# Layer 3's self-attention in a nine-stage transformer kernel: one set of statistics for both norms, one key or query block a unit, other tasks spread out

## The reference, cut to what matters

```
def _layernorm(x, eps=1e-05):
    m = jnp.mean(x, axis=-1, keepdims=True)
    v = jnp.var(x, axis=-1, keepdims=True)
    return (x - m) / jnp.sqrt(v + eps)
# B 8 batches of N 256 tokens, D = 128, H = 16 heads of DK = 8 columns
xx = _layernorm(x)
y = ln1(xx)                                  # again mean and variance, then * ln1_w + ln1_b
q, k, v = split(y @ w_qkv)
attn = softmax(einsum('bhnd,bhmd->bhnm', q, k) * (1.0 / sqrt(DK)))
s = xx + einsum('bhnm,bhmd->bhnd', attn, v) @ w_proj
# a mixture of eight MLPs on s follows, in the next stage
```

## Time and profile before

| | us |
|---|---|
| three runs: median (lowest to highest) | 4559.78 (4558.39 to 4569.89) |
| the profiled execution, its own time | 4569.0 |
| the profiled execution, span from first to last instruction | 4567.2 |
| of it the stage L3s, from its first instruction to its last VectorE instruction | 272 |

### The profile page before, as it was taken

One profiled execution on the slowest core, in us unless ns is written; L12 is line 12 of the kernel. 1 busy time (PEld: TensorE's weight loads), 2 busy tenths in 40 slices (PEclk: granted clock), 3 DMA queues, 4 the chain that ended last, 5 costly groups with the idle time before them and its releaser, 6 DMA issues. The chain is left out here.

```text
span 4567.2 us, 74534 instructions
## 1 busy us (share of the span) xinstructions
PE 4165.2 (91%) x26475; PEld 2849.5 (62%) x26508; DVE 2802.0 (61%) x6502; ACT 2573.6 (56%) x4381; POOL 127.1 (3%) x153
## 2 busy tenths in 40 slices
PE   7797999999789999999999999779999999967889
PEld 6564454454467777777777777446666666644557
DVE  7655888786566665556565555555555555547656
ACT  6423667666256666666666667334444444436457
POOL 2100000000000000000000000000000000000000
PEclk9898999999889999999999999889999999988989
DMA  2101433230110000000000000020000000000010
GB/s 75 51 5 52 68 52 46 48 43 15 37 40 13 5 12 5 15 3 15 2 15 13 4 1 4 24 61 8 9 9 9 9 2 2 2 19 3 8 59 8
DMA packets 118722, 99.10 MB, mean 22 GB/s; under 512 B 12020, under 2 KB 111508, under 8 KB 117244
## 3 DMA queue, kind: packets, MB, share of 16 engines
q1 hardware_dynamic: 112588, 87.28, 8.6%
q10 hardware_dynamic: 5760, 6.92, 0.4%
HBM read 62.85 MB, written 12.58 MB: 17 GB/s over the span
## 5 line engine op out<-in xcount | busy, mean ns | idle before, releaser
L1240 DVE CUSTOM_DVE_ANT_0 L2a_sc<-L2a_score,L2a_mask_n 128x804 f32<-128x804 f32 x512 | 498.9, 991 | 101.1 <-issue 77.7
L1157 ACT ACTIVATE L2a_pt<-L2a_ring 128x512 f32<-128x512 f32 x768 | 431.3, 599 | 203.9 <-PE L2a_ring L1054 202.3
L621 ACT ACTIVATE L1a_work<-L1a_ring 128x1024 f32<-128x1024 f32 x416 | 413.5, 1028 | 173.5 <-PE L1a_ring L439 172.4
L741 DVE TENSOR_REDUCE L1a_mx<-L1a_ring 128x2 f32<-128x1024 f32 x384 | 456.6, 1222 | 66.1 <-PE L1a_ring L458 62.0
L2187 PE MATMUL L3a_res<-L3a_probs,L3a_n 128*128 128x512 f32 (+1 forms) x960 | 489.5, 592 | 0.0
L2280 ACT ACTIVATE L3a_probs<-L3a_ring 128x512 f32<-128x512 f32 (+1 forms) x480 | 279.7, 590 | 309.8 <-PE L3a_ring L2076 305.1
L1054 PE MATMUL L2a_ring<-L2a_ident,L2a_sc 128*128 128x128 f32 x3072 | 443.3, 283 | 5.7 <-ACT L2a_sc L1144 1.9
L1144 ACT ACTIVATE L2a_sc<-L2a_sc,L2a_nb 128x1608 f32<-128x1608 f32 x256 | 417.8, 1634 | 0.7 <-DVE L2a_nb L1245 0.7
L2397 DVE TENSOR_REDUCE L3a_mx<-L3a_ring 128x1 f32<-128x402 f32 (+2 forms) x640 | 316.4, 538 | 152.4 <-PE L3a_ring L2154 143.0
L1054 PEld LDWEIGHTS L2a_ring<-L2a_ident,L2a_sc 128*128 128x128 f32 x3072 | 350.6, 144 | 79.9 <-issue 43.7
L1069 PE MATMUL L2a_res<-L2a_pt,L2a_v 128*64 128x256 f32 (+1 forms) x3328 | 373.4, 381 | 1.7 <-ACT L2a_pt L1157 1.7
(11 more groups left out here) (749 smaller groups left out, 7994.2 us busy)
## 6 DMA issues: line engine op xcount, KB each, us to landing
L1a_keys<-L1a_k_hi SPq DMA_DIRECT2D x224, 52.0 KB
L1a_cx<-in_ctx SPq DMA_DIRECT2D x8, 768.0 KB
L2a_cx<-in_ctx SPq DMA_DIRECT2D x8, 768.0 KB
L1a_keys<-L1a_k_lo SPq DMA_DIRECT2D x112, 52.0 KB
L0a_cx<-in_ctx SPq DMA_DIRECT2D x16, 320.0 KB, 3.5
L3a_cx<-in_ctx SPq DMA_DIRECT2D x16, 320.0 KB, 3.8
L2a_mask_u<-in_mask SPq DMA_DIRECT2D x16, 200.1 KB, 4.4
L1a_scr_q<-L1a_keys SPq DMA_DIRECT2D x3, 1024.0 KB
```

The source lines that it names most:

```text
L621: act.activation(probs[:, (par * NU + u) % c.PS, :, :], ring[tile][:, :, :], ACT.Exp).then_inc(tile_free[tile], 1)
L741: dve.tensor_reduce(mx[:, g % 2, hf, one, :, ch], ring[tile][:, :, :], AX, ALU.max).then_inc(tile_free[tile], 1)
L1157: ins = act.activation(pt[:, t:t + 4, g // 3, q], bank[:, :].rearrange("p (t q) -> p t q", t=4), ACT.Copy)
L1240: dve.tensor_tensor_reduce(sc[:, two, e, w].rearrange("p (k j) -> p k j", k=2), score[e][:, :, 0:CH], mask_n[:, r % 2, w].rearrange("p (k ...
```

## The change

It has these parts:

- Statistics of `x` are taken once, block by block. From mean and variance GpSimd works out both factors: `1/sqrt(var + EPS)` for `xx`, and for `y` in one step `1/sqrt(var * (1 + EPS) + EPS * EPS)`, which is what two norms in a row come to. `norm` writes `y` directly from `x`. `xx` is written by GpSimd in a new task `resid`, a batch at a time, when `finish` will soon want it.
- Blocks 1, 2 and 3 get their statistics and `norm` at different times: block 1 in units 0 and 1, block 2 in 5 and 6, block 3 in 13 and 14.
- `key` and `query` have no part on VectorE any more; that part is a task of its own, `key_lo` or `query_lo`, which stands in the next unit, behind `rows`. From unit 8 on there is one projection a unit, in units 2 to 5 also, and two in units 6 and 7.
- Ahead of unit 0 only groups 0 to 2 of block 0 are projected; group 3 and `value` of block 0 stand in unit 0.
- The tasks of a finished batch stand ahead of `rows` instead of at the third places: `denominator`, `spread (b, 0)`, `spread (b, 1)`, `project` in one unit each, and `finish` in the next one.
- Clearing `v` moves from VectorE to GpSimd, and VectorE takes block 0's statistics ahead of its wait for the weights.

```diff
 def __init__(self):
...
-        for s in ("stats", "rsqrt", "norm", "stats_2", "rsqrt_2", "norm_2"):
+        for s in ("stats", "scale", "norm", "turn"):
             put(s, 0)
-        put("turn", 0)
-        for g in range(self.NG):
+        for g in range(3):
             put("key", (0, g))
             put("query", (0, g))
...
+        for g in range(2):
+            put("key_lo", (0, g))
+            put("query_lo", (0, g))
+        put("tops", (0, 0))
+        put("tops", (0, 1))
+        put("shift", 0)
+        put("key_lo", (0, 2))
+        put("query_lo", (0, 2))
         put("rows", 0)
...
+    def projected(self, u):
+
+        block, at = divmod(u, 8)
+        if u < 0 or block + 1 == self.NB:
+            return []
+        n = block + 1
+        if block:
+            return [(("key", "query")[at % 2], (n, at // 2))]
+        return {2: [("key", (1, 0))], 3: [("query", (1, 0))], 4: [("key", (1, 1))], 5: [("query", (1, 1))],
+                6: [("key", (1, 2)), ("query", (1, 2))], 7: [("key", (1, 3)), ("query", (1, 3))]}.get(at, [])
...
+        b, step = divmod(u - 5, 4)
+        if step == 0 and b >= 1:
+            first.append(("finish", b - 1))
         if b >= 0:
-            tasks += [[("denominator", b)], [("spread", (b, 0))], [("spread", (b, 1)), ("project", b)], [("finish", b)]][(u - 5) % 4]
-        share = lambda k: [put(*t) for t in tasks[k * len(tasks) // 3:(k + 1) * len(tasks) // 3]]
+            first += {0: [("denominator", b), ("resid", b)], 1: [("spread", (b, 0))], 2: [("spread", (b, 1))], 3: [("project", b)]}[step]
+        if n < self.NB:
+            if at == (0 if block else 2):
+                first.append(("turn", n))
+            if at == 6:
+                first.append(("value", n))
+        second += [(kind + "_lo", k) for kind, k in self.projected(u - 1)]
+        if u == 0:
+            second.append(("stats", 1))
+        elif at == 5 and n + 1 < self.NB:
+            second.append(("stats", n + 1))
+        third += self.projected(u)
+        if u == 0:
+            third += [("scale", 1), ("key", (0, 3)), ("query", (0, 3)), ("value", 0), ("key_lo", (0, 3)), ("query_lo", (0, 3))]
+        if u == 1:
+            third.append(("norm", 1))
+        if n + 1 < self.NB and at in (5, 6):
+            third.append((("scale", "norm")[at - 5], n + 1))
...
         put("scores", (u, 0))
-        share(0)
+        share(first)
         if u + 1 < self.NU:
             put("rows", u + 1)
+        share(second)
...
         put("scores", (u, 1))
-        share(1)
+        share(third)
         if ahead:
             put("shift", u + 2)
-        share(2)
...
+            def scale_of(n):
+
+                t = tokens_of(n)
+                pool.wait_ge(mv_ok, n + 1)
+                pool.tensor_scalar(var[:, 1, :], mv[:, t, 1], 1.0 + EPS, EPS * EPS, ALU.mult, ALU.add)
+                pool.tensor_scalar(var[:, 0, :], mv[:, t, 1], EPS, None, ALU.add)
+                pool.drain()
+                pool.tensor_tensor(inv[:, 1, t], var[:, 1, :], half[:, :], ALU.pow)
+                pool.drain()
+                pool.tensor_tensor(var[:, 1, :], mv[:, t, 0], inv[:, 1, t], ALU.mult)
+                pool.drain()
+                pool.tensor_scalar(off[:, t], var[:, 1, :], -1.0, None, ALU.mult).then_inc(scale_ok, 1)
+                pool.tensor_tensor(inv[:, 0, t], var[:, 0, :], half[:, :], ALU.pow)
+                pool.drain()
+                if n == 0:
+                    pool.memset(v[:, :, :], 0.0)
...
+            def resid(b):
+                for t in range(SH * b, SH * (b + 1)):
+                    ins = pool.tensor_scalar(xx[:, t, :], x[:, t, :], mv[:, t, 0:1], inv[:, 0, t:t + 1], ALU.subtract, ALU.mult)
+                ins.then_inc(xx_ok, 1)
...
             dve.memset(parts[:, :, :, :, :, :], 0.0)
-            dve.memset(v[:, :, :], 0.0)
...
```

More of the change, by code:

```diff
@@ L1333, in __init__ @@
             self.unit(u)
-        for what in (("finish", B - 2), ("values", self.NU - 1), ("result", self.NU - 1), ("denominator", B - 1), ("spread", (B - 1, 0)),
-                     ("spread", (B - 1, 1)), ("project", B - 1), ("finish", B - 1)):
+        for what in (("project", B - 2), ("values", self.NU - 1), ("result", self.NU - 1), ("denominator", B - 1), ("resid", B - 1), ("finish", B - 2),
+                     ("spread", (B - 1, 0)), ("spread", (B - 1, 1)), ("project", B - 1), ("finish", B - 1)):
             put(*what)
@@ L1342, in unit @@
         block, at = divmod(u, 8)
-        tasks = []
-        if u < 3:
-            tasks += [[("stats", 1), ("rsqrt", 1), ("norm", 1)], [("stats_2", 1), ("rsqrt_2", 1)], [("norm_2", 1), ("turn", 1)]][u]
-        if block + 1 < self.NB and (u >= 3 or block):
-            n = block + 1
-            prep = [("turn", n)] if block else []
-            for g in range(self.NG):
-                prep += [("key", (n, g)), ("query", (n, g))]
-            prep.append(("value", n))
-            first, steps = (0, 6) if block else (3, 3)
-            k = at - first
-            if k < steps:
-                tasks += prep[k * len(prep) // steps:(k + 1) * len(prep) // steps]
-        b = (u - 5) // 4
-        if b >= 0:
-            tasks += [[("denominator", b)], [("spread", (b, 0))], [("spread", (b, 1)), ("project", b)], [("finish", b)]][(u - 5) % 4]
-        share = lambda k: [put(*t) for t in tasks[k * len(tasks) // 3:(k + 1) * len(tasks) // 3]]
+        n = block + 1
+        first, second, third = [], [], []
+        b, step = divmod(u - 5, 4)
+        if step == 0 and b >= 1:
+            first.append(("finish", b - 1))
+        if b >= 0:
+            first += {0: [("denominator", b), ("resid", b)], 1: [("spread", (b, 0))], 2: [("spread", (b, 1))], 3: [("project", b)]}[step]
[16 more added lines that the diff above has]
+            third.append((("scale", "norm")[at - 5], n + 1))
         ahead = u + 2 < self.NU
+        share = lambda tasks: [put(*t) for t in tasks]
         if ahead:
@@ L1677, in project @@
                 free(act.activation(ft[:, :], bank[:, 0:S], ACT.Copy), "project", b)
-            run(dict(norm=norm, norm_2=norm_2, turn=turn, key=key, query=query, value=value, scores=scores, result=result,
+            run(dict(norm=norm, turn=turn, key=key, query=query, value=value, scores=scores, result=result,
                       project=project))
@@ L1809, in _ @@
             dve.memset(parts[:, :, :, :, :, :], 0.0)
-            dve.memset(v[:, :, :], 0.0)
-            dve.drain()
-            dve.memset(v[:, :, 0:c.H * c.VE].rearrange("p t (h e) -> p t h e", e=c.VE)[:, :, :, c.DH], 1.0)
-            dve.wait_ge(w_in, 16 * (len(loads) + 1))
-            dve.tensor_copy(ident_b[:, :], ident[:, :])
-            dve.tensor_scalar(wq[:, :, :], wq[:, :, :], c.DH ** -0.5, None, ALU.mult)
-            dve.drain()
-            dve.nop().then_inc(const_ok, 1)
-            run(dict(stats=stats, rsqrt=rsqrt, stats_2=stats_2, rsqrt_2=rsqrt_2, key=key, query=query, tops=tops, shift=shift, rows=rows,
-                      denominator=denominator, spread=spread, finish=finish))
+            run(dict(stats=stats, key_lo=key_lo, query_lo=query_lo, tops=tops, shift=shift, rows=rows, denominator=denominator, spread=spread, finish=finish))
 class LatentPlan:
```

83 lines of the change are left out of this document (30 added, 53 removed).

## The result

The changed kernel takes 4537.46 us (median of five runs, 4531.52 to 4546.35), the kernel before 4565.14 on the same chip (five runs, 4558.39 to 4569.89): the ratio is 0.9947, with a 95% interval from 0.9929 to 0.9965 (the two medians by themselves give 0.9939). It is 0.5 to 0.6% faster, where 0.68% was forecast; 4537 lies in the range of 4518 to 4544. The profiled execution took 4531.52 us, with a span of 4529.7.

A forecast was written before the change was run, and what follows sets the result against it. No engine was taken to be full; in-order waits make up the stage, with VectorE pacing settled units. Terms -12.0, -1.9, -16.0, -2.0 and +1.0 (last units and tail) sum to -30.9 us, giving 4529 us, 0.68% faster; range 4518 to 4544.

The forecast's parts named there:

- `yt` earlier: Stage start: `turn` and all behind it come 12.0 us earlier, or 7.5 if `x` came only with the weights, 4.4 later.
- from `yt` to the first addition: Ahead of unit 0: group 3's query and key leave the way to the first addition, -1.9 us.
- units 0 to 8: First addition to the one in unit 8: 59.5 us against 75.45, so -16.0, with ends -8.0 and -19.6.
- two eight-unit blocks: Settled units: waits for `queries` go, other work stands ahead of `rows`; -2.0 us for both, ends -7.4 and +2.
- last units: Last six additions: without projections, tasks ahead of `rows` cost more than behind `shift`; +5.6 us.
- tail: From the last addition to the stage's end: `finish (6)` and two waits leave the way of `values (31)`; -4.6 us.
- the walk: Units 0 to 8 reckoned unit by unit at full clock, 55.9 us in sum; 59.5 was taken to allow for half clock.
- rival (c): Settled blocks: granted clock stays at half, +35 us a block, kernel slower; decides from some 46 us at half clock; chance 0.03.
- signs of being wrong: `x` late, half clock beyond 4115, eight settled units over 54, or reductions waiting behind `denominator` with `values` at twice its duration.
- (a): Only the start is gained; units 0 to 8 gain a third, blocks get +2 or worse: -14, 4546; chance 0.15.
- (b): All waits go and nothing collides: -41 us, 4519 or a little better; chance 0.12 for better than -39.
- (d): Factors come late, GpSimd's chain on each block's path, 2.5 to 3.6 us four times: 4540; no chance of its own.

The follow-up runs named there:

- late_x: The changed kernel with VectorE taking block 0's statistics only behind its wait for the weights; stage 254.0 us against 245.5.
- before_third: The changed kernel with batch tasks behind the second `scores`, ahead of the projection and `shift`; `turn` and `value` stayed ahead of `rows`; stage 242.9 us against 245.5.
- last_late: The changed kernel with batch tasks moved from ahead of `rows` to behind `shift` from unit 25 on; stage 242.3 us against 245.5.
- all_late: The changed kernel with batch tasks moved from ahead of `rows` to behind `shift` from unit 5 on; stage 225.7 us against 245.5.
- lo_later: The changed kernel with the VectorE piece in `denominator` units behind the second `scores` instead of behind `rows`; stage 247.0 us against 245.5.
- after_rows: The changed kernel with batch tasks right behind `rows` instead of ahead of it; `turn` and `value` stayed ahead; stage 243.0 us against 245.5.
- late_to_29: The changed kernel with batch tasks behind `shift` in units 5 to 29, ahead of `rows` in 30 and 31; 4520.1 us, ratio 0.9888 to the kernel before.

## Why the prediction was right, and where its terms were off

| step | predicted | measured |
|---|---|---|
| `yt` earlier | -12.0 | -11.6 |
| from `yt` to the first addition | -1.9 | -1.8 |
| units 0 to 8 | -16.0 (59.5) | -16.4 (59.0) |
| two eight-unit blocks | -2.0 | -1.7 (+1.7, -3.5) |
| last units | +5.6 | +5.5 |
| tail | -4.6 | -5.1 |
| sum | -30.9 | -31.1 |

The total within 0.2 us is in part luck: each side is a single execution, and a fall of the clock in one and not in the other moves a part by 1 to 3 us (late_x's last units are 2.5 us longer than those after the change, with the same order). That each of the six terms came within 0.5 is the better evidence, and two of them hold offsets, as follows.

**The start.** `x` was estimated at 2.9 us behind its issue and came at 3.0, GpSimd's chain at 2.5 and took 2.6. late_x shows the share of VectorE's order, 3.9, where the prediction held 4.4 between its two cases.

**Units 0 to 8.** From second reduction to second reduction, as in the walk: 3.5 to unit 0's first (predicted 3.5), units 0 and 1 13.6 (13.3), unit 2 6.7 (4.4), units 3 to 7 4.3, 4.9, 8.0, 6.2, 6.9 (4.4, 5.0, 8.4, 6.5, 7.3), and 5.0 into unit 8 (3.1). The granted clock was at half up to 4091.4 and again in two short stretches, the last from 4101.7 to 4105.0 (`values` took 1.94 us at 4102.06 and 1.07 at 4107.12). That is 17 of the 59 us, where a mean of 0.71 in the kernel before is some 44 of 75. On the prediction's scale, whose stage starts 6.5 us later, it ended at 4111.5, short of the 4115 named. The 3.6 us put on the full-clock walk for it were about right in size (the walk falls 3.1 short), but not in place. Units 0 and 1, most of them at half clock, lose 0.3; unit 2 loses 2.3, half of it at half clock; and unit 8 loses 1.9 at full clock, where the addition waited 1.6 for `rows` behind `project` and `turn`. So a part of the agreement is offset.

**The blocks.** Predicted 7.1, 7.1, 6.2, 5.5, 6.6, 8.4, 6.9, 5.5; measured in the first block 7.6, 7.8, 7.0, 5.3, 6.1, 8.1, 6.3, 5.4, and in the second, without `stats`, 6.6, 7.0, 6.0, 5.3, 6.1, 6.9, 6.3, 5.4. In the first block's second and third unit the clock had fallen to 0.50 behind `denominator` (the windows above): they took 1.9 us more than the same two of the second block. That is rival (c) on a small scale: the block had some 10 us at half clock (4146.0 to 4152.9 and 4173.3 to 4176.8) instead of the 46 from which it would have decided. Two of the prediction's signs of being wrong did show, though too briefly to decide anything: half clock beyond 4115, and `values` at twice its length behind a `denominator`. The first unit took 1.0 more than that of the second block: unit 7 had projected a key and a query, so unit 8 finishes both (three VectorE pieces, 2.15 us from 4140.66 on) where unit 16 has the query's two, and the sum had only the query there. What the sum removed was 4.2 us of waiting for `queries` a block (8.3 in both); the reductions' 10.9, which shrank to 1.2, were not a term of their own. The estimate of 1.1 us for a key beside the multiplication was 1.25 in the blocks ((11.7 - 9 x 0.745) / 4), and up to 1.29 singly (2.04 against 0.75). Here the Trainium skill's "SBUF — State Buffer", section "Who interferes with whom", was right on every count that the runs show: two inputs in SBUF collide (also at 4240.16 in the kernel before, 1.54 us), `TENSOR_REDUCE` doesn't (1.19 us at 4121.91, beside `resid` on GpSimd; it reads PSUM here), and the engine that comes second waits until the other's instruction has ended. The same section says that `tensor_scalar` on one input can take the shared ports too, in a fast mode; the 1.99 us of `parts` in before_third agree with that.

**The last units and the tail** came as costed. They were put down as the price of tasks ahead of `rows` with no projections to hide them; last_late confirms it (6.9 us back there, 3.8 given away in the tail).

**Rivals.** (a) fell: units 0 to 8 gained 16.4, and the blocks gained too. (b) did not happen: its waits would have gone, but collisions and the wait for `rows` took their place; all_late shows what that was worth. (d) fell: the factors are waited for at the stage's start only; ScalarE's `norm` of blocks 1 to 3 waits for nothing (0.0 us).

**The time.** The stage's gain was met within 0.2 us; the median's was 27.7 where 31 was forecast. The rest is scatter of the untouched stages, which moved single executions by 10 us and more, and that 4529 was reckoned from a median of three runs (4559.78) which five runs put at 4565.14: from that, the same sum gives 4534.

**What was missed** lies outside the sum. Each place of a task has its price on each engine in turn, and for the blocks the prediction costed one place only: placed behind `shift`, the same work takes 19.8 us less, 24.2 with the tail's order changed too. Why the places between give the blocks back only 4.8 and 6.8 of the 13.4 us is shown in part: ahead of `rows` the addition waits (8.8 us), right behind `rows` the reductions do (7.7), ahead of `shift` the reductions (4.2) and `shift` itself beside GpSimd (6.9).

## What to carry to other kernels

- In a pipeline of in-order engines, look for the place of side work where the engine would otherwise idle: here behind the last hand-over of a unit, not ahead of the small product that the next engine waits for. Read it from the groups by line: a small instruction with a large idle time before it (here the addition, 0 us before and 8.8 after) names the place that is wrong, and moving the blame from one line to another without shortening the unit (lo_later, and after_rows in part) suggests that the cause is further up.
- A collision of VectorE and GpSimd hits the next VectorE instruction that can collide; moving one can hand it to another (key, then `shift`). Give the work to an engine with room, or let it fall beside reductions.
- A wait of TensorE can cost more than its length, if the products behind it run at half clock. Filling one wait of 1.9 us with products that were due anyway shortened the tail by 4.5 us, 1.8 of them because the products behind ran at full clock. Look at the granted clock of the products behind a wait before you price it.

## What the runs showed of the hardware

- TensorE's granted clock fell from 1.00 to 0.50 at sixteen four-column products in a row (at 4144.95, 2.42 us), in a window in which its records show no gap (in the 5.9 us ahead of it TensorE was busy for 4.62): `values` then took 1.94 us instead of 1.07. It did so behind some of these groups and not behind others of the same kernel (at 4118.00 `values` took 1.07).
- In late_to_29 the clock fell from 1.00 to 0.50 within a wait of TensorE of 2.09 us (it was 1.00 up to 4261.2 and 0.50 from 4261.3, the wait ended at 4261.86).
- Two VectorE `TENSOR_SCALAR` of 128x4 from one SBUF input, 0.25 us together by themselves, took 1.99 beside a GpSimd multiplication of 1.91 us: they waited for nearly the whole of it.
- GpSimd's subtraction and multiplication of a 128x128 tile (`resid`) took 0.8 us alone and 1.24 (at 4149.74) beside a key of VectorE.
